# Token blocks in a new order on all engines, with the second gate in one pass and no block 64

## The reference

```python
x1 = layernorm(x)
q, k, v = (x1 @ W + b for Wq, Wk, Wv)                      # 16 heads of 32
alpha = 0.9 * sigmoid(silu(x1 @ Wg1 + bg1) @ Wg2 + bg2) + 0.1   # Wg1: 512 -> 16, Wg2: 16 -> 512
intra = softmax(causal(q k^T / sqrt(32))) v                 # inside chunks of 64 tokens
inter_t = q_t S;  S = alpha_t * S + k_t v_t^T               # a scan over all tokens
x = x + inter + intra
x2 = layernorm(x)
probs = softmax(x2 @ router_w.T); top 8 of 64, renormalised; at most 256 tokens per expert
x = x + sum over a token's experts (silu(x2 Wg) * (x2 Wu)) Wd + shared expert of width 384
```

## Time and profile before

| what | us |
|---|---|
| median of 3 runs | 4608.77 (4606.50 to 4610.91) |
| the profiled execution's own time | 4610.58 |
| its span, first to last instruction | 4608.7 |
| busy: PE / DVE / ACT / POOL | 4433.4 / 3520.7 / 2271.6 / 1333.8 |
| last matrix product of the tokens' phase starts | 3678.34 |
| first matrix product of the experts' phase starts | 3711.65 |

### The profile page before, as it was taken

One profiled execution on the slowest core, in us unless ns is written; L12 is line 12 of the kernel. 1 busy time (PEld: TensorE's weight loads), 2 busy tenths in 40 slices (PEclk: granted clock), 3 DMA queues, 4 the chain that ended last, 5 costly groups with the idle time before them and its releaser, 6 DMA issues. The chain is left out here.

```text
span 4608.7 us, 182901 instructions
## 1 busy us (share of the span) xinstructions
PE 4433.4 (96%) x74416; PEld 3859.5 (84%) x74416; DVE 3520.7 (76%) x7639; ACT 2271.6 (49%) x7475; POOL 1333.8 (29%) x1275
## 2 busy tenths in 40 slices
PE   6999999999999999999999999999999969999998
PEld 5888888888888888888888888888888769999998
DVE  5777777777777777777777777777777778888887
ACT  4444444444444444444444444444444446666665
POOL 2111111111111111222221111111111156666666
PEclk9999999999999999999999999999999989999999
DMA  2001001011010001000001000001010079999997
GB/s 67 32 31 31 31 31 36 32 35 33 31 31 32 32 31 32 32 31 31 32 32 35 31 31 32 31 31 36 32 36 32 32 242 266 270 265 270 267 267 194
DMA packets 195037, 358.24 MB, mean 78 GB/s; under 512 B 16736, under 2 KB 92896, under 8 KB 194352
## 3 DMA queue, kind: packets, MB, share of 16 engines
q1 hardware_dynamic: 160848, 269.47, 17.6%
q0 software_dynamic: 33632, 79.73, 7.8%
HBM read 243.87 MB, written 107.50 MB: 76 GB/s over the span
## 5 line engine op out<-in xcount | busy, mean ns | idle before, releaser
L591 ACT ACTIVATE PR<-PR,MX 128x64 f32<-128x64 f32 x2048 | 682.7, 335 | 736.6 <-DVE MX L1186 736.6
L477 POOL TENSOR_TENSOR RI<-PV,AL 128x512 f32<-128x512 f32 x65 | 78.7, 1212 | 2448.5 <-DVE PV L1140 2448.5
L729 PE MATMUL bank<-XTh,wsguh 128*128 128x256 f32 x1536 | 447.1, 291 | 0.1
L1678 PE MATMUL ebank<-XH,WH 128*128 128x256 f32 x1536 | 431.3, 281 | 7.3 <-DVE XL L1760 7.3
L730 PE MATMUL bank<-XTl,wsguh 128*128 128x256 f32 x1536 | 430.4, 280 | 0.0
L731 PE MATMUL bank<-XTh,wsgul 128*128 128x256 f32 x1536 | 430.4, 280 | 0.0
L1678 PE MATMUL ebank<-XH,WL 128*128 128x256 f32 x1536 | 429.8, 280 | 0.0
L1678 PE MATMUL ebank<-XL,WH 128*128 128x256 f32 x1536 | 429.6, 280 | 0.0
L1753 DVE TENSOR_TENSOR WL<-WS,WH 128x768 fp32r<-128x768 f32 (+1 forms) x455 | 370.8, 840 | 16.2
L591 ACT ACTIVATION_READ_ACCUMULATOR PR<-PR,MX 128x1 f32 x2048 | 383.0, 187 | 0.0
L1615 ACT ACTIVATE WH<-WS 128x768 fp32r<-128x768 f32 (+1 forms) x455 | 325.2, 747 | 26.6 <-DMA WS<-in_L_ffn_w_down_dram 26.6
(11 more groups left out here) (228 smaller groups left out, 13243.6 us busy)
## 6 DMA issues: line engine op xcount, KB each, us to landing
WS<-in_L_ffn_w_gate_dram SPq DMA_DIRECT2D x65, 768.0 KB
WS<-in_L_ffn_w_up_dram SPq DMA_DIRECT2D x65, 768.0 KB
WS<-in_L_ffn_w_down_dram SPq DMA_DIRECT2D x65, 768.0 KB
norm_rows<-XR SPq DMA_DIRECT2D x64, 576.0 KB, 3.5
X<-in_L_attn_x_dram SPq DMA_DIRECT2D x66, 512.0 KB, 3.7
out_dram<-X SPq DMA_DIRECT2D x64, 512.0 KB, 2.9
CR<-token_counts,count_at POOLq DMA_INDIRECT x136
XG<-norm_rows,row_at POOLq DMA_INDIRECT x132, 6.2
```

Source lines behind the costliest of these rows:

```text
L477: nc.gpsimd.tensor_tensor(inverse[:, :, 0:half], PV[:, :, :], running[:, :, HC:half:-1], ALU.mult).then_inc(folded.sem, 1)
L591: ins = nc.scalar.activation(PR[b][:, j, :], PR[b][:, j, :], ACT.Exp, bias=MX[b][:, j:j + 1], scale=1.0, accum_out=SU[b][:, j:j + 1])
L729: nc.tensor.matmul(out, sh, mh, start=first, stop=False)
L1678: last = nc.tensor.matmul(bank[HID[m]][:, a * CAP:(a + 1) * CAP], w, x[odd][:, c, :], start=(c == 0 and i == 0), stop=(c == KC - 1 and i = ...
```

## The change

- Router and shared expert get turned rows of their own, XB[0] and XB[1]; XT is left to the first normalisation. KD now lies in RI's buffer, s1 in t1's.
- The columns of Wg1 and the rows of Wg2 are laid out three times, at partitions 0, 32 and 64 (`COPIES`). ACT writes the high part of s1 over all of `sg` (`s1_high`), DVE writes the low part over its rows 32 to 63 (`s1_low`); wg2 holds high, high and low. So one f32r product of 256 columns gives high*high + low*high + high*low; before it was one product in plain float32.
- Every engine's list of work is in a new order. Scores 0, 1 and 2 of the next block are now made inside the step, before the shared expert's down product, and the projections stand in fewer and longer runs. `softmax_a` is split (`scores_part`, `decay_part`), `residual` gives its second half to `variance2`, `route_b` its second half to `route_rows`, `router` is `router_high` and `router_low`. The banks are given out anew (`JOBS`: bank, and how many blocks ahead).
- The lists end with block 63, written out; nothing is made for blocks 64 and 65. ACT, DVE and POOL loop over 62 blocks, PE loops over 48 and has 14 more behind.

```diff
-BANK_OF = {"G1": 3, "Qa": 0, "G2a": 2, "G2b": 3, "Ka": 0, "Qb": 1, "Kb": 2, "ATr0": 3, "V0": 0, "V1": 1, "ATr1": 2,
-           "X2Ta": 3, "X2Tb": 0, "KTok0": 2, "RL": 1, "KTok1": 3, "GU0": 2, "RLT": 1, "GU1": 0, "GU2": 3, "DK": 1,
-           "DN0": 2, "DN1": 0}
+JOBS = {
+    "Ka": (2, 1), "Kb": (0, 1), "ATr0": (1, 0), "Qb": (3, 1), "V0": (1, 1), "V1": (0, 1), "ATr1": (2, 0), "X2Ta": (3, 0),
+    "X2Tb": (2, 0), "RL": (3, 0), "GU0": (2, 0), "RLT": (3, 0), "KTok0": (0, 1), "KTok1": (0, 1), "GU1": (2, 0), "DK": (0, 1),
+    "GU2": (3, 0), "G1": (2, 2), "Qa": (3, 2), "DN0": (1, 0), "DN1": (3, 0), "G2a": (1, 2), "G2b": (0, 2)}
...
-        wg2 = sb("wg2", [GP, DIM])
+        wg2 = sb("wg2", [GP, DIM], f32r)
+        XB = [sb(f"XB{i}", [P, KC, TB], f32r) for i in "hl"]
-        s1 = sb("s1", [GP, TB])
+        s1 = t1
+        sg = sb("sg", [GP, TB], f32r)
-        KD = sb("KD", [P, KC, TB])
+        KD = RI
...
+            def s1_high(t):                      # ACT
+                act.wait_ge(s1_made.sem, t.value(s1_made))
+                act.wait_ge(g2_filled.sem, t.value(g2_filled, back=1))
+                nc.scalar.activation(sg[:, :], s1[:, :], ACT.Copy).then_inc(s1h_ready.sem, 1)
+            def s1_low(t):                       # DVE
+                dve.wait_ge(s1h_ready.sem, t.value(s1h_ready))
+                v.tensor_tensor(sg[32:64, :], s1[32:64, :], sg[32:64, :].bitcast(f32), ALU.subtract).then_inc(s1_ready.sem, 1)
...
-                    last = nc.tensor.matmul(..., wg2[:, m * P:(m + 1) * P], s1[:, :], start=True, stop=True)
+                    last = nc.tensor.matmul(..., wg2[:, m * P:(m + 1) * P], sg[:, :], start=True, stop=True)
```

PE's list in the loop, after the change (n is the next block, m the one after it; K, Q, V are parts of projections, each of 12 products of 256 columns or, for V, 3 of 512):

```diff
+            def step(t):
+                turn_probs(t, 1); K(n, 0, part 0); outputs(t, 0); scores(t, 3); outputs(t, 1)
+                K(n, 1, part 0); turn_out(t, 0); K(n, 0, part 1); turn_probs(t, 2); K(n, 1, part 1); outputs(t, 2)
+                turn_probs(t, 3); Q(n, 1, part 0); V(n, 0, 1 chunk); outputs(t, 3); V(n, 1, 1 chunk); turn_out(t, 1)
+                V(n, 1, 1 chunk); Q(n, 1, part 1); V(n, 0, 2 chunks); x2t(t, 0); V(n, 1, 1 chunk); x2t(t, 1)
+                V(n, 0, 1 chunk); V(n, 1, 1 chunk); router_high(t); router_low(t); gate_up(t, 0); turn_logits(t)
+                ktok(n, 0); scores(n, 0); ktok(n, 1); gate_up(t, 1); state_updates(n, 0); state_updates(n, 1)
+                xt(m, 0); xt(m, 1); gate_up(t, 2); scores(n, 1); positions(t); gate1(m); turn_probs(n, 0)
+                Q(m, 0, both parts); down(t, 0, all 3); down(t, 1, all 3); gate2(m, 0); gate2(m, 1); scores(n, 2)
```

The lists of the other engines in the loop (DVE, ACT, POOL), in the same shorthand:

```diff
+ DVE: decays(n) scores_part(t,3) softmax_b(t,2) products(n) residual(t,0) weights(t,2) decay_part(t,3) softmax_b(t,3)
+      variance2(t,0) weights(t,3) inverse(n,0) inverse(n,1) residual(t,1) variance2(t,1) norm2(t,0) norm2(t,1)
+      x2t_low(t,0) x2t_low(t,1) values(n,0) values(n,1) norm1(m) route_a(t) hidden(t,0) shift1(m) scores_part(n,0)
+      decay_part(n,0) route_b(t) hidden_low(t,0) hidden(t,1) state(n,0) xt_low(m,0) xt_low(m,1) hidden_low(t,1)
+      hidden(t,2) softmax_b(n,0) scores_part(n,1) state(n,1..3) silu1(m) hidden_low(t,2) route_c(t) decay_part(n,1)
+      weights(n,0) total(t,0) s1_low(m) softmax_b(n,1) route_rows(t) total(t,1) scores_part(n,2) weights(n,1) decay_part(n,2)
+ ACT: q_evac(n,0) gate2(n,0) gate2(n,1) alpha(n) ot(t,0) exp(t,2) ot(t,1) exp(t,3) ot(t,2) k_evac(n,0) k_evac(n,1)
+      ot(t,3) q_evac(n,1) x2t(t,0) x2t(t,1) lt(t) gu(t,0) ktok_evac(n,0) router_exp(t) ktok_evac(n,1) normalise(m)
+      hidden_high(t,0) gu(t,1) exp(n,0) xt_evac(m,0) xt_evac(m,1) hidden_high(t,1) gu(t,2) hidden_high(t,2) gate1(m)
+      exp(n,1) s1_high(m)
+ POOL: fold(t) decayed_k(t) decayed_q(t) rstd1(n) rstd2(t,0) unpair(n) rstd2(t,1)      # t, n as POOL's own step counts
```

More of the change, by code:

```diff
@@ L33 @@
 GH = 16
+COPIES = (0, 32, 64)
 GP = 128
@@ L601, in ot, with x2t @@
                                      ACT.Copy).then_inc(ot_evac.sem, 1)
[L603 to L608, removed]
+            def x2t(t, k):
+                act.wait_ge(gu_filled.sem, t.value(gu_filled, back=1))
+                act.wait_ge(x2t_filled.sem, t.value(x2t_filled, k))
+                nc.scalar.activation(XB[0][:, 2 * k:2 * k + 2, :], bank_of("X2Ta" if k == 0 else "X2Tb")[:, :]
+                                     .rearrange("p (a b) -> p a b", a=2), ACT.Copy).then_inc(x2h_ready.sem, 1)
             def hidden_high(t, m):
@@ L668, in _ @@
-            normalise(t.next())
-            xt_evac(t.next())
-            with act.Fori(0, NBLK // 2) as pair:
-                for odd in range(2):
[L672 to L702, removed]
+            act.wait_ge(w_low, len(staged) + 2)
@@ L992, in _ @@
[L992 to L1018 removed]
+            pe.wait_ge(rw_ready, 5)
@@ L1054, in feed @@
                 down(t, 1, (2,))
-                positions(t)
-            def step(t):
-                feed(t)
-                attend(t.next())
-            attend(first)
-            with nc.Fori(0, PE_LOOPED // 2, PE_BODY // 2, engines=[pe.engine], hint_back_edge=True) as pair:
-                for odd in range(PE_BODY):
+                gate2(m, 0)
+                gate2(m, 1)
+                scores(n, 2)
+            xt(Turn(0, 0), 0)
+            xt(Turn(0, 0), 1)
+            gate1(Turn(0, 0))
@@ new lines, in _ @@
+            state_updates(Turn(0, 0), 1)
+            xt(Turn(0, 1), 0)
+            xt(Turn(0, 1), 1)
+            scores(Turn(0, 0), 1)
+            gate1(Turn(0, 1))
+            turn_probs(Turn(0, 0), 0)
+            project(Turn(0, 1), 0, wq, q_filled, ("Qa", "Qb"))
+            gate2(Turn(0, 1), 0)
+            gate2(Turn(0, 1), 1)
+            scores(Turn(0, 0), 2)
+            with nc.Fori(0, 24, 8, engines=[pe.engine], hint_back_edge=True) as pair:
+                for odd in range(16):
@@ L1065, in _ @@
                     step(Turn(pair, odd))
-            for odd in range(PE_LOOPED, NBLK - 1):
+            for odd in range(48, 62):
                 step(Turn(0, odd))
-            feed(Turn(0, NBLK - 1))
+            turn_probs(Turn(0, 62), 1)
+            project(Turn(0, 63), 0, wk, k_filled, ("Ka", "Kb"), parts=(0,))
+            outputs(Turn(0, 62), 0)
+            scores(Turn(0, 62), 3)
+            outputs(Turn(0, 62), 1)
+            project(Turn(0, 63), 1, wk, k_filled, ("Ka", "Kb"), parts=(0,))
@@ new lines, in _ @@
+            gate_up(Turn(0, 62), 0)
+            turn_logits(Turn(0, 62))
+            ktok(Turn(0, 63), 0)
+            scores(Turn(0, 63), 0)
+            ktok(Turn(0, 63), 1)
+            gate_up(Turn(0, 62), 1)
+            state_updates(Turn(0, 63), 0)
+            state_updates(Turn(0, 63), 1)
+            gate_up(Turn(0, 62), 2)
+            scores(Turn(0, 63), 1)
+            positions(Turn(0, 62))
+            turn_probs(Turn(0, 63), 0)
+            down(Turn(0, 62), 0, (0, 1))
+            down(Turn(0, 62), 0, (2,))
@@ new lines, in _ @@
+            down(Turn(0, 62), 1, (0, 1))
+            down(Turn(0, 62), 1, (2,))
+            scores(Turn(0, 63), 2)
+            turn_probs(Turn(0, 63), 1)
+            outputs(Turn(0, 63), 0)
+            scores(Turn(0, 63), 3)
+            outputs(Turn(0, 63), 1)
+            turn_out(Turn(0, 63), 0)
+            turn_probs(Turn(0, 63), 2)
+            outputs(Turn(0, 63), 2)
+            turn_probs(Turn(0, 63), 3)
+            outputs(Turn(0, 63), 3)
+            turn_out(Turn(0, 63), 1)
+            x2t(Turn(0, 63), 0)
@@ L1319, in _ @@
                             rwT[:, :, 0:E].bitcast(f32), ALU.subtract).then_inc(w_low, 1)
[L1320 to L1334 removed]
+            dve.wait_ge(rw_ready, 2)
@@ new lines, in _ @@
+                    links[0], links[1] = 0, Turn(pair, odd)
+                    step(Turn(pair, odd))
+                    assert links[0] == LINKS, links[0]
+            links[0], links[1] = START + 62 * LINKS, None
+            decays(Turn(0, 63))
+            scores_part(Turn(0, 62), 3)
+            softmax_b(Turn(0, 62), 2)
+            products(Turn(0, 63))
+            residual(Turn(0, 62), 0)
+            weights(Turn(0, 62), 2)
+            decay_part(Turn(0, 62), 3)
+            softmax_b(Turn(0, 62), 3)
```

670 lines of the change are left out of this document (443 added, 227 removed).

## The result

The changed kernel takes 4522.99 us (median of 4 runs, 4515.84 to 4531.44) against 4608.94 us before (4 runs, 4606.50 to 4610.91): a ratio of 0.9817, 95% interval 0.9805 to 0.9829. It is faster by 1.8%, where 6.1% was forecast: 86 us instead of 282, and outside the range. The profiled execution took 4525.55 us, span 4523.8.

A forecast was written before the change was run, and what follows sets the result against it. PE's list was taken as the bound: 53.5 - 1.33 - 0.84 + 0.25 = 51.6 us, plus 0.5 of waits. 83.5 + 62 x 52.1 + 80.5 = 3394, 284 less, gave 4326, with 1 for the clock 4327 us; range 4285 to 4445.

The forecast's parts named there:

- no wait is forced: Whole steps: at six places operands come 0.1 to 2 us before PE needs them, leaving waits between 0 and 2.8.
- 51.6 plus waits of 0.5: Whole step: 51.6 us of PE work plus 0.5 of waits, a period of 52.1 us.
- The walk: Whole step: PE's new list laid out beside the other engines' lists; it found no forced wait, so 0.5 us taken.
- Start: Prologue: the first whole step begins at 83.5 us, give or take 3, the prologue's work nearly unchanged.
- Tail: After the whole steps: block 62 takes 46 us (5.6 of work gone), block 63 alone 34.6, together 80.5.
- The charge for it: Block 63 alone: a low PE clock throughout would double 13.7 us of products, +14; 1 us was taken.
- The state updates' 0.25: State updates back to back: the second waits for the first's result, +0.25 us per block, between 0 and 0.4.
- my sum of PE's work: One block's PE groups counted at 53.5 us before, and 51.6 us in the new list.
- It is sure, since nothing hides PE's work: Gate 2 in one pass: 0.48 us of products in place of 1.81, so -1.33 us per block.
- (a): PE's waits: the old 2.8 us per block stay, period 54.4, 4469 us; chance 0.17.
- (b): POOL's chain before scores 0: GpSimd held up by DVE passes, period 54.9, 4500 us; chance 0.05.
- (c): DVE and ACT become the bound through their order: 7.2 us of waits per block, 58.8, 4742 us; chance 0.05.
- (d): Gate 2 still at the plain rate and block 64's products still made: 4430 us; chance 0.03 with things unnamed.

The follow-up runs named there:

- e5: The changed kernel with e1's separators, e2's earlier and halved stores, and XN's first transposes between the two state updates; 4376.09 us, ratio 0.9500.
- e8: e1 with gate 2's operands kept in plain f32 instead of f32r, the copy and subtraction staying; 4480.72 us, ratio 0.9724.
- e3: The kernel before with only gate 2 in one f32r pass and the three list moves it needs; 4610.73 us, ratio 1.0005.
- e2: The changed kernel with normalised rows made and stored some 4 us earlier and the output's store halved, PE's list untouched; 4457.41 us, ratio 0.9673.
- e7: The changed kernel with only the store of the normalised rows started about 13 us later, behind the row of small products; 4459.77 us, ratio 0.9675.
- e1: The changed kernel with f32r products of K moved between outputs 0, scores 3 and outputs 1 to break up the row; 4389.26 us, ratio 0.9528.
- e6: The changed kernel with one separator: K's part 0 moved between outputs 0 and scores 3, scores 3 and outputs 1 left together; 4439.96 us, ratio 0.9640.

## Why the prediction was wrong

**The step that failed** is "no wait is forced", and with it the period "51.6 plus waits of 0.5". The walk laid PE's list beside the other engines' lists and looked for whoever comes late. It put at nothing the time that PE's own instructions take to come (1.41 us of stops per step), and what PE's clock does then (1.33 us per step). The profiled execution took 4525.55, the forecast's sum was 4326. The account of the 199 us:

- Whole steps, +174 (62 x (54.91 - 52.1)). Stops of 1.41 us per step: 87 us. Low clock: a step of an f32r run takes 0.213 instead of 0.119 us there, so 0.44 of the low time is lost, 187.7 x 0.44 = 83 us. That leaves 4 us. With both taken off a step is 52.2, against 52.1 forecast.
- Start, +8.5: the first whole step begins at 91.99. Gate 2 of block 0 is 3 us later than before, and the low stretch of the prologue is 17.1 us instead of 13.7, worth 1.5. The other 4 us are not traced; taking one gate 2's place for another step's beginning is part of it.
- Tail, +16.4: the rest lasts 96.9 us, not 80.5. Block 62's step took 52.1, not 46; block 63 alone 45.0, not 34.6. Its timeline shows both causes, waits at about the places that the working gave, and groups at twice their length:

```profile
3552.64 0.67 PE L901 MATMUL sa<-QD,RI 32*32 32x64 f32 x32 [2.17 <-DVE AM L1343]
3553.24 1.13 PE L915 MATMUL sa<-KT,QT 32*64 32x64 f32 x32
...
3571.15 2.10 PE L993 MATMUL bank<-ident,XR 128*128 128x128 f32 x8 [2.54 <-DVE XR L1384]
3574.30 1.22 PE L1003 MATMUL bank<-XBh,rwT 128*128 128x256 f32 x4 [1.04 <-DVE XBl L1433]
```

The clock was low from 3551.6 to 3578.9. The charge for it was named as 1, up to 14; the upper end was right: 27.3 us x 0.44 = 12. The Trainium skill, "TensorE: Matmul & The Clock Gate", section "What's actually happening", was weighed for just this, and the trace agrees with it (0.70 over block 63's 45 us). In block 62's step the fault is another: without the products of a block 64 there is less cover, and in e5, where the clock is up, PE waits 0.57 for the probabilities and 1.56 for down's last operand, so the 5.6 us of work gave 2.8.

**What held.** The groups kept 0.36, 1.30 and 1.36; gate 2's products are 0.12 apart; DVE's busy time is 2608.98 / 62 = 42.1 per block (42.5 forecast); from the last product of the tokens to the first of the experts it is 33 us as before. The state updates' 0.25 is there as a wait of L881 on itself. The floor of e5 is 52.07 with no wait, and with that wait out and two more changes between runs and small groups in, it should have been 51.6, so my sum of PE's work was 0.45 low, about what I had set aside for waits: the 52.1 came out right from two halves that were each off.

**"It is sure, since nothing hides PE's work"**, said of gate 2, holds in the new order, where no engine makes PE wait (e8: 91 us, where 62 x 1.33 = 82), and failed in the order before, where PE's waits belong to chains of VectorE and ScalarE: there gate 2's part alone gave 0 us (e3), with longer waits in place of the shorter products.

**The rivals.** (a) gives 54.4 per step and 4469, but the waits on engines that it is made of are not there. (b) GpSimd, with 54.9 and 4500, is nearest in number, and that is chance: PE waits for nothing of it. POOL's busy time per step is 704.33 / 62 = 11.4, against 11.1 in the earlier trace rows, so nothing held it up by the 2.8 us that this rival needed. By the Trainium skill's rule ("SBUF — State Buffer", section "Who interferes with whom") it could have been held up; the trace shows at most those 0.3 us. (c) and (d) fell: no long engine wait, and the change does what it says. The true one was missing from the list: I gave 0.03 to (d) and things unnamed together.

**What is shown, and what is argued.** Shown: the stop stands inside a group with nothing to wait for; it returns at the same instruction with the loop's body; it ends some 1.4 us after a packet of instructions has landed, and from stop to stop PE uses 256 instructions per packet; it goes when f32r products are put into the row, and comes when such a row is made in the old kernel; the stores beside it lengthen it. So it is the bringing of instructions. The sizes fit: 526 packets start in the 62 whole steps, 8.5 each. The row uses 448 instructions in 3.96 us, so a packet of 256 in 2.3 us (an f32r run takes 15), while those packets that end a stop take 0.96 us in the median, and PE goes on 1.4 us later, 2.4 us together. The Trainium skill, "Trainium Architecture — The Big Picture", section "The software stack", has instructions of 64 bytes, so a packet would hold 256, as the count from stop to stop gives. It also says that the streams are brought to the engines when the program is loaded; the traffic of that queue during the run shows that here they come while it runs.

Not shown is how the stores lengthen the stop. Whether the clock would fall without the stop was not separated either: of 52 steps of the change with a gap of over 0.9 us in the row, 14 have no fall (18 of 37 in e2, 17 of 41 in e7), so the stop doesn't always bring it. The loop's ends still cost time in e5, 55.7, 55.5 and 61.0 us instead of 52.1; gaps of 3.3 to 3.7 us stand there, and they too end 1.5 to 1.8 us after a packet has landed.

## What to carry to other kernels

When an order of work is laid out by hand, check a third thing beside the engines' shares and the waits: the number of instructions per microsecond that TensorE's list asks for, over several microseconds; put long products between groups of small ones. A gap with the releaser "issue" in the middle of a group, at a place that returns with the loop's body, is the mark of it; the granted clock behind it is the second half of the bill. And ask of each microsecond taken from the busiest engine whether its waits would not simply grow: here the saving came through where the engine had no waits on others, and was lost where it had some.

## What was not expected of the hardware

- TensorE stops for 0.7 to 2.3 us within a row of 448 instructions in 3.96 us; rows of up to 192 instructions (e1) left 0.11 us per step, rows of up to 328 (e6) 0.21. Each stop ends about 1.4 us after a 16 KB packet of instructions has landed.
- A store of 576 KB moved away from such a row, with nothing else touched, gave 63 us (14 per thousand of the time); with the row broken up, moving the stores gave nothing that could be told apart.
- A stop of 0.9 to 3.1 us in a list that is otherwise dense came, in 39 of 62 steps, with 3.4 to 10.2 us of low clock (3.4 in 31 of them), while the kernel before, with 2.8 us of waits per block in small pieces, kept 2.4 GHz throughout its blocks.
